# A decoder layer on one core: the feed-forward weights' rounding moved from cross attention into self attention

## The reference

```python
scalers_1 = jnp.max(jnp.abs(blocks), axis=1)
...
scaled = (blocks / scalers_1[:, None]).reshape(-1)
idx = jnp.argmin(jnp.abs(scaled[:, None] - NF4), axis=-1)
...
w1 = nf4_roundtrip(weight1)
w2 = nf4_roundtrip(weight2)
w3 = nf4_roundtrip(weight3)
...
x = _layernorm(x + _L0_attn_ref(x, ...), axis=-1)
x = _layernorm(x + _L0_xattn_ref(x, ctx_512, ...), axis=-1)
x = _layernorm(x + _L0_ffn_ref(x, w1, w2, w3), axis=-1)
```

## Time and profile before

| | us |
|---|---|
| median of 3 runs | 1098.47 (1096.72 to 1100.58) |
| the profiled execution | 1099.43 |
| its span, first to last instruction | 1097.7 |
| self attention, steps of batches 0 to 3 | 39.7 to 471.4 |
| cross attention, steps of batches 4 to 7 | 471.4 to 821 |
| feed-forward layer | to the end |

### The profile page before, as it was taken

The page is one execution under the profiler, slowest core; times in us unless marked ns, Lnnn a source line. Parts: engine busy times, 40 slices in busy tenths (PEclk is TensorE's granted clock), DMA queues, the critical chain, the costliest instruction groups (busy, mean ns, idle before and its releaser), DMA issues.

```text
span 1097.7 us, 17718 instructions
## 1 busy us (share of the span) xinstructions
PE 1036.2 (94%) x6280; PEld 671.9 (61%) x6280; DVE 752.9 (69%) x1684; ACT 486.9 (44%) x587; POOL 432.0 (39%) x462
## 2 busy tenths in 40 slices
PE   9999999999999889999889998999999999999995
PEld 7555554554555355556456555655647888888884
DVE  7789759666866679658866976897775645463635
ACT  4444344654465556555754765586451212111110
POOL 3548565986588444322342333233266000000000
PEclk9899899999999899999989999999999999999998
DMA  6741576387646864747565575748537203010021
GB/s 233 226 103 27 131 196 188 101 230 189 184 111 154 219 172 124 167 104 166 165 165 144 131 191 149 166 130 189 133 69 240 82 1 116 1 42 36 0 77 39
DMA packets 92618, 145.17 MB, mean 132 GB/s; under 512 B 22506, under 2 KB 39794, under 8 KB 92274
## 3 DMA queue, kind: packets, MB, share of 16 engines
q1 hardware_dynamic: 83218, 116.49, 40.9%
q0 software_dynamic: 8000, 26.75, 8.5%
q10 hardware_dynamic: 1312, 0.79, 0.3%
HBM read 78.09 MB, written 23.73 MB: 93 GB/s over the span
## 4 chain that ended last, share of the span: by engine, by line
PE 54%; DVE 10%; DMA 5%; issue 4%; POOL 4%; ACT 3%; SPq 1%; DVEq 0%; ACTq 0%; POOLq 0%
PE att_pv L1043 9%; PE att_pv L1303 7%; PE att_scores L1303 7%; PE att_scores_T L1333 7%; PE att_scores_T L1016 5%; PE att_scores L982 5%; PE att_scores_T L968 4%; PE att_scores_T L970 4%; PE att_scores_T L969 4%; DVE att_scores L1671 2%; DMA att_q_stack<-att_m_rows 1%; DVE att_nf_zone L1831 1%; PE att_scores_T L1165 1%; DMA att_probs<-nf_x 1%; ACT att_probs L1474 1%
## 5 line engine op out<-in xcount | busy, mean ns | idle before, releaser
L1474 ACT ACTIVATE att_probs<-att_scores_T 128x1024 f32<-128x1024 f32 (+2 forms) x256 | 218.3, 883 | 148.5 <-PE att_scores_T L1016 144.7
L1043 PE MATMUL att_pv<-att_probs,att_v 128*32 128x512 f32 (+3 forms) x1024 | 217.0, 540 | 1.8 <-POOL att_probs L845 1.6
L1043 PE MATMUL att_pv<-att_probs,att_ones 128*32 128x512 f32 (+3 forms) x1024 | 216.9, 540 | 0.0
L1677 DVE TENSOR_REDUCE att_mx<-att_scores 128x1 f32<-128x512 f32 x248 | 159.1, 683 | 79.7 <-PE att_scores L982 78.5
L982 PE MATMUL att_scores<-att_k_stack,att_q_stack 96*128 96x256 f32 (+1 forms) x504 | 171.4, 405 | 10.2 <-DVE att_mx L1677 6.1
L1016 PE MATMUL att_scores_T<-att_q_stack,att_k_stack 97*128 97x512 f32 (+2 forms) x512 | 143.7, 391 | 13.6 <-DVE att_nf_zone L1845 4.9
L1671 DVE CUSTOM_DVE_ANT_0 att_scores<-att_scores,att_cmask 128x128 f32<-128x128 f32 (+3 forms) x256 | 121.0, 511 | 39.3 <-PE att_scores L982 37.5
L845 POOL TENSOR_SCALAR_AFFINE_SELECT att_probs<-att_probs 128x256 f32<-128x256 f32 x128 | 58.0, 453 | 220.9 <-ACT att_probs L1474 217.3
L982 PEld LDWEIGHTS att_scores<-att_k_stack,att_q_stack 96*128 96x128 f32 x504 | 90.3, 193 | 55.2 <-DVE att_mx L1677 20.0
L1016 PEld LDWEIGHTS att_scores_T<-att_q_stack,att_k_stack 97*128 97x128 f32 x512 | 88.2, 195 | 55.3 <-DVE att_nf_zone L1845 17.7
L1570 ACT ACTIVATE att_probs<-att_scores 128x512 f32<-128x512 f32 x44 | 26.3, 598 | 207.4 <-PE att_scores L1303 207.4
(11 more groups left out here) (262 smaller groups left out, 2091.1 us busy)
## 6 DMA issues: line engine op xcount, KB each, us to landing
att_q_stack<-att_q_hi SPq DMA_DIRECT2D x128, 128.0 KB, 3.4
att_probs<-nf_x SPq DMA_DIRECT2D x28, 352.0 KB, 3.6
att_nf_home<-nf_reciprocals POOLq DMA_DIRECT2D x48, 176.0 KB, 4.7
att_q_stack<-att_q_lo SPq DMA_DIRECT2D x64, 128.0 KB, 3.6
att_k_stack<-att_k_hi SPq DMA_DIRECT2D x64, 128.0 KB, 3.5
att_nf_home<-nf_x SPq DMA_DIRECT2D x20, 352.0 KB, 3.7
w_nf<-att_nf_zone SPq DMA_DIRECT2D x192, 22.0 KB, 2.5
att_k_stack<-att_k_hi SPq DMA_DIRECT2D x64, 64.0 KB, 3.4
```

Of the source, the lines that this page charges most:

```text
L1043: last = T.matmul(pv[HD * j:HD * j + HD, sums, q0:S], lhs, pr[:, at:at + S - q0], start=(t == 0), stop=(t == TT - 1))
L1474: A.activation(probs_of(b, r)[:, 1024 * h:1024 * h + w], bank[:, 0:w], ACT.Exp, scale=SCALE).then_inc(st_free, 1)
L1677: V.tensor_reduce(mx[:, p % 2, TT * r + t:TT * r + t + 1], sco[:, r, :], AX.X, ALU.max).then_inc(sc_free, 1)
```

## The change

Rounds per step (a number of steps in brackets where the batches differ):

| | before | after |
|---|---|---|
| batches 1, 2: steps 2, 3, 4, 6 | 1 each | 2 each |
| batch 3, step 3 | 1 | 2 |
| batches 4 to 6: steps 2, 4, 5 | 1 each | none |
| all other steps | | unchanged |

So 9 rounds leave cross attention and 9 enter self attention, and the last round stays in step (7, 1). Passes on ScalarE go from 65 to 57, on VectorE from 127 to 135: a doubled step has passes 1 and 2 of `mid` and pass 1 of `end` on ScalarE; elsewhere pass 0 alone is there. The four buffers rotate: pass 0 of round u writes the buffer that round u + 1 loads from, so that the next transfer may go when the first quarter of the sums (`first_sums`, which bumps `first_summed`) has read its buffer four loads before; the first pass of a round now also waits for the whole round before. In a doubled step TensorE does both parts of `weigh`, then the first sums of `mid`, then the first half of the projection, the rest of `mid`, the second half and `end`, and VectorE's passes are placed to suit. In cross attention steps 1 to 6 the first sums of the round go ahead of `weigh`.

```diff
-SELF_ROUNDS = 20
+SELF_ROUNDS = 29
...
+def doubled(b, p):
+
+    return 0 < b < B - 1 and p in (2, 3, 4, 6) or (b, p) == (B - 1, 3)
...
-            if b < B and p == 5 or b == B - 1 and p > 4 or (b, p) in ((1, 0), (B, 0)):
-                continue
-            steps += [(b, p)] * (2 if p == 1 and b > 1 else 1)
+            if b < B:
+                none = p == 5 or b == B - 1 and p > 4 or (b, p) == (1, 0)
+            else:
+                none = p in (2, 4, 5) or (b, p) == (B, 0)
+            if not none:
+                steps += [(b, p)] * (2 if p == 1 and b > 1 or doubled(b, p) else 1)
...
-    if crossed(b):
-        return (0, 1) if p in (2, 4, 5) else (0,)
-    return (0, 1, 3) if b < B - 1 and p in (3, 4) else (0,)
+    if doubled(b, p):
+        return (1, 2) if u + 1 < ROUNDS and ROUND_STEPS[u + 1] == (b, p) else (1,)
+    return (0,)
...
+        def rows_and_passes(u):
+
+            four = [home(u)[0]] + over
+            turned = four[u % 4:] + four[:u % 4]
+            return turned[0], turned[1:] + turned[:1]
...
-                x4, dqb = home(u)
+                x4 = rows_and_passes(u)[0]
                 if u > 0:
-                    sp.wait_ge(st_full, AT["round", u - 1] + 1)
+                    sp.wait_ge(first_summed, u)
...
+            def first_sums(u):
+
+                bank_for(("round", u))
+                if 0 in scalar_passes(u):
+                    pe.wait_ge(over_act, ACT_PASSES[u] + 1)
+                else:
+                    pe.wait_ge(over_vec, VEC_PASSES[u] + 1)
+                sums_of_pass(u, 0).then_inc(first_summed, 1)
...
+                    if doubled(b, p):
+                        weigh(b, p, 1)
+                        first_sums(mid)
...
+                        if doubled(b, p):
+                            rounding(mid, True)
                         make(b + 1, whats, 1)
...
+                    begun = end is not None and crossed(b) and 0 < p < 7
+                    if begun:
+                        first_sums(end)
...
+                    if u > 0:
+                        dve.wait_ge(st_full, AT["round", u - 1] + 1)
...
+                    if doubled(b, p):
+                        if p % 2 == 0:
+                            over_sums(G)
+                        exceeds(mid, (3,))
+                    else:
                         exceeds(end, (1, 2))
...
+                    if doubled(b, p):
+                        scale_rounded(mid)
+                        exceeds(end, (0, 2, 3))
+                    else:
+                        exceeds(end, (3,))
```

61 lines of the change are left out of this document (34 added, 27 removed).

## The result

The changed kernel takes **1131.53 us** (median of 4 runs, 1125.93 to 1133.55) against 1099.36 for the kernel before in the same comparison: ratio 1.0283, 95% interval 1.0247 to 1.0320, **31 us slower** by that ratio (27 to 35). The forecast was 1097.5 with a range up to 1111. The profiled execution of the changed kernel took 1129.93 us.

The account below looks back on a forecast made before the run. TensorE, busy 94% of the span, was taken as the bound, held back by VectorE in cross attention. 1099.4 - 21.3 (cross attention) + 21.4 (self attention) - 1.0 (steps 1) = 1098.5, less 1.0 for the median: 1097.5 us, range 1084 to 1111.

Parts of the forecast that it names:

- The empty steps of cross attention: Steps 2, 4 and 5 of batches 4 to 6, losing their rounds, give back 11.3 us together.
- step 3: Cross attention: starts with less VectorE backlog and its input landed, 0.8 us less each, 2.4 in all.
- the two later steps 6: Cross attention, (5,6) and (6,6): earlier loads shorten each by about 0.7 us, 1.4 together.
- a doubled step by itself costs 0.55: Self attention: the layout of one doubled step reaches the second pair of scores at 10.7 us, against 10.15 before.
- +3.0: Steps 3 and 4 of batches 1 and 2: us added to each by the queue's bound, 12.0 in all.
- The matmuls: Self attention: nine added rounds at 0.60 us each, 5.4 us that nothing hides.
- a run of passes waits once: Doubled steps: a group of VectorE passes waits for GpSimd's port only once, charged 0.8 us per group.
- The queue's loop: Doubled steps in a row: store, stacks, load and passes allow one every 16.6 us, or 17.4 with a port wait.
- The sign named for it: Steps 3 and 4, batches 1 and 2: 17.5 us, ScalarE and VectorE waiting for a load issued behind the stacks.
- A: Self attention absorbs the added rounds, steps 3 and 4 paying some 1.2 us rather than 3: 1085.7 us; chance 0.30.
- B: GpSimd's port sets the doubled steps, 2.2 us per group instead of 0.8 in four steps: 1108.7 us; chance 0.21.
- C: Cross attention: rotation brings loads no earlier and (4,6) keeps its wait: 1105.1 us; chance 0.14.

Follow-up runs that it names:

- e5: The change, but in cross attention a round's first sums come behind the weighing again; 1.0260 of the kernel before.
- e8: The change, but only steps 2 and 6 of batches 1 and 2 doubled, only steps 5 and (4,4) of cross attention emptied; 1.0165 of the kernel before.
- e16: The change with eight useless matmuls ahead of the first sums in the nine doubled steps; 1.0376 of the kernel before.
- e4: The change, but in self attention from step 2 on, the load of a step's first round is issued ahead of the stack transfers; 1.0230 of the kernel before.
- e1: The change's buffer rotation and early first sums alone, with rounds and ScalarE's share of passes as in the kernel before; 1.0012 of that kernel.
- e3: The change with GpSimd's rotary turning in self attention on 64 of 512 columns, leaving out most of it; 1.0175 of the kernel before.
- e12: The kernel before with rotating buffers, only (3,3) doubled, (5,5) emptied, and some reordered loads, sums and passes; 1.0017 of the kernel before.
- e17: The kernel before with rotating buffers, one round each moved into (1,5) and (2,5) from (5,5) and (6,5), cross attention's first sums behind the weighing; 1.0091.
- e14: The change with doubled steps' passes on 176 of 1408 columns and self attention's first-round loads ahead of the stacks; 1.0193 of the kernel before.
- e15: The kernel before with GpSimd's turning on 64 of 512 columns, leaving out most rotary turning; 0.9939 of the kernel before.

## Why the prediction was wrong

**The empty steps of cross attention**: right. 4.0 + 3.3 + 4.0 = 11.3 forecast; measured 4.0 for steps 2, 1.4 for steps 4 and 4.8 for steps 5, 10.2. Steps 4 got less since (4,4) stayed at 9.3 us, with a clock dip new in it. (4,6) fell by 3.3 (2.8 forecast), of which some 2 by the earlier issue and the rest by a faster landing, which is luck; steps 7 fell by 2.9 (3.0). Wrong were step 3 (2.4 forecast, 0.2 measured: the backlog ahead of it had cost nothing) and the two later steps 6, forecast 0.7 shorter each and in fact 1.8 and 3.0 longer. Sum 12.0 instead of 21.3.

**Self attention**: the failed step. "So a doubled step by itself costs 0.55", and on it "+3.0", "+1.7", "+1.3" and "+2.0", 21.4 together, less 1.0 in steps 1. Measured: 45.1. By steps, in us, with e5 as the second execution of the same self attention:

| steps | forecast | the change | e5 |
|---|---|---|---|
| (1,3), (1,4), (2,3), (2,4) | +12.0 | +27.9 | +18.2 |
| (1,2), (2,2) | +3.4 | +4.2 | +5.5 |
| (1,6), (2,6) | +2.6 | +2.3 | +3.6 |
| (1,7), (2,7) | +1.4 | +4.5 | +5.4 |
| (3,3) | +2.0 | +4.7 | +2.8 |
| (1,5), (2,5) | no term | +4.4 | +4.4 |
| (1,1), (2,1), (3,1) | -1.0 | -3.8 | -1.1 |
| the others | no term | +0.9 | +2.7 |

Single steps scatter, but in both executions the failure lies first in the +3.0 for each of steps 3 and 4 (4.6 to 7.0 measured), then in the steps behind doubled ones: 7 was priced too low, and 5, which had no round and got no term, pays 2.2 each (it stays at 8.3 in e8, where steps 4 are not doubled). Steps 2 and 6 came near the forecast. Term by term:
- The matmuls: 5.4 forecast at 0.60 a round, 10.1 measured, 1.1 a round.
- The waits: 16.0 forecast (21.4 - 5.4), 23.1 of idle time measured. The layout of one step was right up to the first round's scaling (7.0 forecast, 7.3 measured in (1,3)). Behind it 0.8 was charged for a group's wait at GpSimd's port, where the second round's three passes took 5.9 us instead of 1.8: "a run of passes waits once" did not hold. The price was read too low from the trace of before: "the other passes in self attention took 0.58" is wrong, since 6 of the 52 in batches 1 to 3 took 1.5 to 2.8 us. For the landing 3.6 was taken, the median of all loads, where (2,3) had 7.5.
- The clock: 0 forecast, 12.0 us of longer matmuls measured. How much of that a higher clock alone would give back, e16 leaves open.
- The queue's loop of 16.6 to 17.4 us, of which "this bound, not VectorE's or TensorE's work, sets steps 3 and 4" was said. Measured from one first pass of `mid` to the next: 22.5 into (1,4), 20.4 into (2,3), 21.5 into (2,4). The sign named for it, TensorE and the passes waiting for a load issued behind the stacks, was there in (2,3). But the loop is not all that makes a doubled step dear. e4, which takes the stacks out of it, gave 6 us; e8, where no two doubled steps follow each other, still paid 4.6 a step.
- The gain in self attention's steps 1, forecast 1.0, was 3.8 in this execution; e1, with the same rotation, has (1,1) at 23.6 us against 19.9, and e5 gained 1.1 in steps 1, so it is scatter as much as gain.

**The rivals.** A fell: nothing was absorbed. B (the port) had the sign and the place, but its 1108.7 took 2.2 us for two groups in four steps; and e3 with its control leaves it some 5 us of doubled steps, with an error of 9. C was right in what it says of the rotation by itself (e1, no gain), wrong in (4,6), which the emptied step and a faster landing shortened. The range failed with them: every case took the doubled step as a sum of single costs, each with its cover, and none had a term for a step behind it that holds no round.

**What is shown and what is open.** Shown: the loss lies in self attention and comes with each round more that it gets, doubled or single, some 4.2 to 5.0 us each by the windows of single executions (e8, e12, e17, the change; over its whole stretch e17 paid 11.3 for two), against 1.1 us a round given back by an empty step of cross attention. Shown too: none of the causes that were varied carries it alone. The passes' length (7 us), the load's place (6, not clear of noise), GpSimd's large instructions (12, 5 of them the doubled steps', not clear of noise), the first sums' place (none) and VectorE's share (none) were changed one by one, and 21 us stay with short passes and the load ahead (e14). Open: no run has short passes, small turns and the load ahead together, and e14's passes still waited for GpSimd, so the share of the port in these 21 us is not known. Argued and not shown: that the rest is the number of hand-overs as such. A round more in an otherwise full step is one more chain of load, passes, sums, bank and scaling through five engines that each work in order, and the wait that one edit removes appears at the next. A run that takes the chain itself away (buffers and a bank of its own for each round) was not tried.

No version beat the kernel before: e1 and e12 are level with it. e15 is faster but does not do the work.

## What to carry to other kernels

Before moving work between stages, move one or two units and measure them in both places, by windows: here (e17) a round cost 4.7 us in the new step and saved 1.8 in the old one, though VectorE and ScalarE had idle time in the new one. Don't price an added round in a full step by its matmuls alone (0.60 us here): look at each wait that its chain of load, passes, sums and scaling adds, and at the steps behind. Read all instructions of a kind and not their median when some wait: the median pass was unhindered before and after (0.58 and 0.59 us), and the mean of those in the doubled steps 1.2. And take a control for an edit that leaves work out: e3 alone would have given the port 12 us, and the control took more than half of it back.
